# First self attention of a two-layer decoder: queries projected two units ahead, rotated sums rounded one unit later, written-out orders for VectorE and ScalarE

## The chip, the cores and the metric

One Trainium2 chip, one of its cores. The metric is device time in microseconds of one execution of the whole program. A core has a matmul engine (TensorE, in the profile PE, with its weight loads as PEld), VectorE (DVE), ScalarE (ACT), GpSimd (POOL) and SyncE (SP), each with a queue of its own that runs in order; they meet only by semaphores. DMA transfers are started from SyncE and GpSimd.

## What is computed

A decoder of two layers on x of 2 x 512 tokens of 512 features. Each sublayer is followed by adding its input and a layer norm. In order: causal self attention with rotary embedding (the subject here), cross attention to 1024 context rows with RMS norms, an expert MLP, causal self attention, grouped cross attention, and an MLP with weights and activations quantised to fp8 steps. All 16 heads have 128 features.

```python
q = split_heads(x @ Wq); k = split_heads(x @ Wk); v = split_heads(x @ Wv)
q = _apply_rope(q, cos, sin); k = _apply_rope(k, cos, sin)
scores = jnp.einsum('bhqd,bhkd->bhqk', q, k) * scale
scores = jnp.where(causal, NEG_INF, scores)
attn = jax.nn.softmax(scores, axis=-1)
ctx = jnp.einsum('bhqk,bhkd->bhqd', attn, v)
return ctx @ Wo
```

## The kernel before

Every product is made in float32 quality out of bfloat16 parts: an operand is kept as a high part and a low part (hi, lo), and `three()` issues three matmuls, hi by hi, hi by lo, lo by hi (lines 1272 to 1274). ScalarE writes a hi part as a rounded copy, VectorE the lo part as a difference.

**Units.** Attention goes by units: one head of one batch row, 32 in all, two batch rows of a head after each other. A unit has four quarters `qt` of 128 queries; since the mask is causal, quarter `qt` has 128 (qt + 1) keys. Its steps for a quarter: the score on TensorE into one of two score banks; VectorE adds mask and scale and takes the minimum (`scores`, L1187; it writes `p` and `nb`); ScalarE takes the exponential with its row sum (L892); VectorE the reciprocal (`inverse`, L1196); ScalarE the normalised hi part (`rounded`, L881, writes `phl`); VectorE its lo part (`remainder`, L1206); SyncE starts one DMA transpose of both (L463, it lands in `pT`, a part of `wo`), and TensorE multiplies them by v (`weigh`). `units()` (line 225) writes units 0 to 3 and 28 to 31 out and puts the 24 between in a loop of four.

**Jobs.** The projections of later units are jobs in slots between the quarters of a unit: `slots = [("Q",), ("K",), (), ("V",)]` (line 74). Their two banks in PSUM are taken in turn: a job waits for VectorE's part of the job two before it (`job_lo`). `lead(kind)` says how many units ahead a job works: before, 2 for K and 1 for Q and V. The rotation of a Q or K job passes through three engines: ScalarE copies the two halves of the bank crosswise to `swap` (L832, L833), VectorE multiplies the bank by the cosine into `rot` (L1143), GpSimd multiplies `swap` by the sine (L661) and adds it to `rot` (`rope`, L664, counted by `rope_sum`). Then `rotated` writes the hi part on ScalarE (L861, counted by `rope_hi`) and the lo part on VectorE (L1159, counted by `rope_lo`). Before, K's is done in the next unit, Q's at the end of quarter 1 of the same unit.

**Orders.** ScalarE and VectorE walk through the quarters with `unit()`, all by one pattern: VectorE does reciprocal of the last quarter, score, remainder of the last quarter, parts of the job; ScalarE does rounding of the last quarter, exponential, parts of the job. TensorE: score 0, Q, weighting of quarter 1 of the last unit, score 1, K, weighting of quarter 2, score 2, score 3, weighting of quarter 3, V, weighting of the unit's own quarter 0.

**Weights.** GpSimd splits raw weights into hi and lo: key and value weights of a head (`wkv`, L551 and L556) in quarter 0 of every odd unit, ahead of Q's rotation; the query weight (`wq`) in quarter 1, behind K's rotation (`split_plan`, line 91, and GpSimd's `unit`, line 671). The end of `wq_lo` counts `w_split`, for which the job of that head waits (`job`, line 1379: `pe.wait_ge(w_split, head(n + lead) + 1)`). SyncE loads the raw weights in even units, behind the transpose of quarter 0. From unit 29 on GpSimd splits the output weights `wo` instead.

## Time and profile before

| | before |
|---|---|
| median of 3 runs (lowest to highest) | 2615.45 us (2614.6 to 2620.56) |
| profiled execution, its own time | 2614.38 us |
| span of the profiled execution, first to last instruction | 2612.6 us |
| TensorE matmul busy | 2438.2 us (93%) |
| TensorE weight load busy | 1567.4 us (60%) |
| VectorE busy | 1848.3 us (71%) |
| ScalarE busy | 1588.8 us (61%) |
| GpSimd busy | 711.8 us (27%) |
| granted TensorE clock, mean | 0.976 |
| first score of unit 0 of the first self attention | 36.5 us |
| first score of its unit 31 | 435.0 us |

How to read the rows further down: times are microseconds from the first instruction; a timeline row has start, duration, engine, line, operation, output <- inputs with their shapes, and in brackets how long the engine had been idle before it and who ended that. A duration counts from when the engine began with the instruction, so a time in which it was held up inside is part of it. Names of tiles are those of the program without buffer numbers; `wo_hi<-phl` is a transposed softmax tile.

### The profile page before, as it was taken

The page shows a single profiled execution, that of the slowest core. Times are in us where ns is not written, and L with a number is a line of the kernel's source. Part 1 is how long each engine was busy: PE and PEld are TensorE (multiplying, and loading weights), DVE is VectorE, ACT ScalarE, POOL GpSimd, SP SyncE. Part 2 cuts the span into 40 slices and gives each one's busy share as a digit, 9 for nine tenths or more (in the row PEclk, how much of TensorE's full clock was granted, in tenths as well). Part 3 has the DMA queues.
Part 4 walks back from the last instruction along what each step waited for, and adds up shares of the span by engine and source line. Part 5 has one row for each costly group of instructions (what it writes and reads, how often), then busy time and mean ns, then how long its engine had stood idle before and what let it go on. Part 6 is the DMA issues. An engine that isn't in the chain of part 4 may idle for free. (4 is left out here: it accounts for less than half of the span.)

```text
span 2612.6 us, 57672 instructions
## 1 busy us (share of the span) xinstructions
PE 2438.2 (93%) x21584; PEld 1567.4 (60%) x21584; DVE 1848.3 (71%) x3371; ACT 1588.8 (61%) x2718; POOL 711.8 (27%) x671
## 2 busy tenths in 40 slices
PE   7999998989999999999988999999899999999864
PEld 4555555546666666666465666665566666665432
DVE  4777777657777777776665666667578888884597
ACT  5777675158887777886244566553277777773242
POOL 5666665601111111012332222226100000013111
PEclk9999999999999999999988999999999999999987
DMA  2433335325666666667341444445188777777200
GB/s 93 90 76 87 79 82 127 103 55 108 114 118 110 113 109 117 115 108 154 113 169 26 94 93 96 95 93 139 30 146 149 145 147 144 146 149 153 69 1 32
DMA packets 769429, 273.83 MB, mean 105 GB/s; under 512 B 737905, under 2 KB 740721, under 8 KB 767601
## 3 DMA queue, kind: packets, MB, share of 16 engines
q1 hardware_dynamic: 767504, 265.82, 49.0%
q0 software_dynamic: 1760, 5.77, 0.8%
q8 instruction: 110, 1.80, 0.3%
q14 instruction: 55, 0.44, 0.1%
HBM read 84.55 MB, written 6.44 MB: 35 GB/s over the span
## 5 line engine op out<-in xcount | busy, mean ns | idle before, releaser
L881 ACT ACTIVATE phl<-p,ri 128x1024 bf16<-128x1024 f32 (+4 forms) x512 | 437.4, 854 | 414.0 <-DVE ri L1196 386.1
L1206 DVE SCALAR_TENSOR_TENSOR phl<-p,ri,phl 128x1024 bf16<-128x1024 f32 (+4 forms) x512 | 514.1, 1004 | 103.3 <-issue 75.3
L892 ACT ACTIVATE p<-p,nb 128x1024 f32<-128x1024 f32 (+4 forms) x512 | 435.9, 851 | 53.9 <-DVE nb L1189 39.6
L1273 PE MATMUL ps<-wo_lo,v_hi 128*128 128x128 bf16 x2496 | 440.0, 220 | 0.0
L1272 PE MATMUL ps<-wo_hi,v_hi 128*128 128x128 bf16 x2240 | 396.5, 220 | 23.0 <-DMA wo_hi<-phl 15.7
L1274 PE MATMUL ps<-wo_hi,v_lo 128*128 128x128 bf16 x2240 | 396.2, 220 | 0.0
L1272 PE MATMUL ps<-k_hi,q_hi 128*128 128x512 bf16 (+3 forms) x768 | 272.5, 355 | 20.9 <-DVE nb L1187 18.7
L1273 PE MATMUL ps<-k_lo,q_hi 128*128 128x512 bf16 (+3 forms) x768 | 271.9, 354 | 0.0
L1274 PE MATMUL ps<-k_hi,q_lo 128*128 128x512 bf16 (+3 forms) x768 | 271.7, 354 | 0.0
L1273 PEld LDWEIGHTS ps<-wo_lo,v_hi 128*128 128x128 bf16 x2496 | 245.1, 98 | 33.4 <-issue 0.5
L1272 PEld LDWEIGHTS ps<-wo_hi,v_hi 128*128 128x128 bf16 x2240 | 219.5, 98 | 68.0 <-DMA wo_hi<-phl 27.9
L551 POOL TENSOR_SCALAR wkv_hi<-raw_kv 128x1024 bf16<-128x1024 f32 (+1 forms) x56 | 49.2, 878 | 658.9 <-PE ps L1274 509.5
L1274 PEld LDWEIGHTS ps<-wo_hi,v_lo 128*128 128x128 bf16 x2240 | 219.7, 98 | 0.0
L1272 PE MATMUL ps<-xT_hi,wq_hi 128*128 128x512 bf16 x512 | 195.1, 381 | 4.5 <-DVE xT_lo L958 3.5
L1191 DVE CUSTOM_DVE_ANT_0 p<-ps,rk,nq 128x1024 f32<-128x1024 f32 x128 | 163.1, 1274 | 51.3 <-PE ps L1274 51.0
L1273 PE MATMUL ps<-xT_lo,wq_hi 128*128 128x512 bf16 x512 | 195.1, 381 | 0.0
L1274 PE MATMUL ps<-xT_hi,wq_lo 128*128 128x512 bf16 x512 | 195.1, 381 | 0.0
L1272 PE MATMUL ps<-wo_hi,oT_hi 128*128 128x512 bf16 x512 | 194.4, 380 | 0.6 <-DVE nb L1187 0.6
L1273 PE MATMUL ps<-wo_lo,oT_hi 128*128 128x512 bf16 x512 | 194.2, 379 | 0.0
L1274 PE MATMUL ps<-wo_hi,oT_lo 128*128 128x512 bf16 x512 | 194.1, 379 | 0.0
L651 POOL TENSOR_TENSOR nq<-nq,half_neg 128x4 f32<-128x4 f32 x32 | 32.3, 1010 | 549.6 <-DVE nq L1140 549.6
L1189 DVE CUSTOM_DVE_ANT_0 p<-ps,mb 128x1024 f32<-128x1024 f32 x128 | 155.8, 1217 | 36.5 <-PE ps L1274 34.2
(200 smaller groups left out, 6126.5 us busy)
## 6 DMA issues: line engine op xcount, KB each, us to landing
raw_kv<-in_wkvself SPq DMA_DIRECT2D x32, 512.0 KB, 4.0
raw_q<-in_wqself SPq DMA_DIRECT2D x32, 256.0 KB, 2.6
raw_q<-in_woself SPq DMA_DIRECT2D x32, 256.0 KB, 2.8
raw_q<-in_wqcross SPq DMA_DIRECT2D x32, 256.0 KB, 3.0
raw_q<-in_wocross SPq DMA_DIRECT2D x32, 256.0 KB, 3.0
wo_hi<-phl SPq DMA_TRANSPOSE x384, 3.2
wo_lo<-phl SPq DMA_TRANSPOSE x384, 3.1
raw_kv<-in_wkvcross SPq DMA_DIRECT2D x24, 256.0 KB, 3.2
```

The costliest lines, as they stand in the source:

```text
L551: nc.gpsimd.tensor_scalar(hi, src, 1.0, 1.0, ALU.mult, ALU.mult).then_inc(w_hi, 1)
L651: nc.gpsimd.tensor_tensor(r, r, half_neg[:, 0:QT], ALU.pow).then_inc(q_norm, 1)
L881: nc.scalar.activation(m["ph"](qt, w), m["p"][:, qt % 2, 0:w], ACT.Copy, scale=ri[:, qt % 2:qt % 2 + 1]).then_inc(p_norm, 1)
L892: nc.scalar.activation(prob, prob, ACT.Exp, scale=1.0 if L.rms else -1.0, bias=nb[:, qt % 2:qt % 2 + 1], accum_out=rs[:, qt % 2:qt % 2 + 1 ...
L1189: ins = nc.vector.tensor_tensor_reduce(in1=m["mb"][:, L.batch(n), :], scale=-ISQ, op0=ALU.add, **kw)
L1191: ins = nc.vector.tensor_tensor_reduce(in1=m["rk"][:, n % 2, :], scale=m["nq"][:, n % 2, qt:qt + 1], op0=ALU.mult, **kw)
L1206: nc.vector.scalar_tensor_tensor(out=m["pl"](qt, w), in0=m["p"][:, qt % 2, 0:w], scalar=ri[:, qt % 2:qt % 2 + 1], in1=m["ph"](qt, w), op0= ...
L1272: nc.tensor.matmul(o, l(0), r(0), start=first, stop=False)
L1273: nc.tensor.matmul(o, l(0), r(1), start=False, stop=False)
L1274: return nc.tensor.matmul(o, l(1), r(0), start=False, stop=last)
```

## The change

In the first self attention alone (`L.rope`):

- `lead` is 2 for Q too: the job in unit n projects the queries of unit n + 2. The prologue (n = -2, -1) has one Q job more, unit 30 one less.
- `rotated` of both jobs is done in the next unit, on ScalarE and on VectorE. VectorE's cosine product waits first for the `rope_lo` of the unit before.
- ScalarE and VectorE get an order written out, `rotary_unit`, in place of the pattern.
- TensorE weighs quarter 1 of the last unit behind the unit's score 1 rather than ahead of it.
- GpSimd's and SyncE's programs stay as they are, apart from counts that follow from the lead.

```diff
--- before.py
+++ after.py
@@ -79,7 +79,7 @@
 
     def lead(self, kind):
 
-        return 2 if self.rope and kind in ("K",) else 1
+        return 2 if self.rope and kind in ("Q", "K") else 1
 
     def rope_count(self, n, qt):
 
@@ -880,23 +880,42 @@
                     act.wait_ge(r_inv, at(lambda n: c["s"] + QT * n + qt + 1, n, it))
                     nc.scalar.activation(m["ph"](qt, w), m["p"][:, qt % 2, 0:w], ACT.Copy, scale=ri[:, qt % 2:qt % 2 + 1]).then_inc(p_norm, 1)
 
+                def rotary_unit(n, it):
+
+                    if n:
+                        rounded(n - 1, it, 3)
+                    exponential(n, it, 0)
+                    rotated(n - 1, it, 0)
+                    job_parts(n, it, 0, L.jobs(n, 0))
+                    rounded(n, it, 0)
+                    exponential(n, it, 1)
+                    rotated(n - 1, it, 1)
+                    job_parts(n, it, 1, L.jobs(n, 1))
+                    exponential(n, it, 2)
+                    rounded(n, it, 1)
+                    exponential(n, it, 3)
+                    rounded(n, it, 2)
+                    job_parts(n, it, 3, L.jobs(n, 3))
+                    if n:
+                        heads_out(n - 1, it)
+
+                def exponential(n, it, qt):
+
+                    act.wait_ge(s_max, at(lambda n: CREDIT + c["s"] + QT * n + qt + 1, n, it))
+                    prob = m["p"][:, qt % 2, 0:L.width(qt)]
+                    if L.rms:
+                        nc.scalar.activation(nb[:, qt % 2:qt % 2 + 1], m["mx"][:, qt % 2:qt % 2 + 1], ACT.Copy, scale=-1.0).then_inc(max_neg, 1)
+                        act.wait_ge(max_neg, at(lambda n: QT * n + qt + 1, n, it))
+                    nc.scalar.activation(prob, prob, ACT.Exp, scale=1.0 if L.rms else -1.0, bias=nb[:, qt % 2:qt % 2 + 1], accum_out=rs[:, qt % 2:qt % 2 + 1]).then_inc(p_exp, 1)
+
                 def unit(n, it):
                     for qt in range(QT):
                         if n or qt:
                             rounded(*((n, it, qt - 1) if qt else (n - 1, it, QT - 1)))
-                        act.wait_ge(s_max, at(lambda n: CREDIT + c["s"] + QT * n + qt + 1, n, it))
-                        prob = m["p"][:, qt % 2, 0:L.width(qt)]
-                        if L.rms:
-                            nc.scalar.activation(nb[:, qt % 2:qt % 2 + 1], m["mx"][:, qt % 2:qt % 2 + 1], ACT.Copy, scale=-1.0).then_inc(max_neg, 1)
-                            act.wait_ge(max_neg, at(lambda n: QT * n + qt + 1, n, it))
-                        nc.scalar.activation(prob, prob, ACT.Exp, scale=1.0 if L.rms else -1.0, bias=nb[:, qt % 2:qt % 2 + 1], accum_out=rs[:, qt % 2:qt % 2 + 1]).then_inc(p_exp, 1)
-                        if L.rope and qt == 0:
-                            rotated(n - 1, it, 1)
+                        exponential(n, it, qt)
                         job_parts(n, it, qt, L.jobs(n, qt))
                         if qt == QT - 1 and n:
                             heads_out(n - 1, it)
-                        if L.rope and qt == 1:
-                            rotated(n, it, 0)
                         if L.rms:
                             key_norms(n, it, qt, L.jobs(n, qt))
 
@@ -907,11 +926,11 @@
                 for n in (-2, -1):
                     for qt in range(QT):
                         job_parts(n, None, qt, L.jobs(n, qt))
-                        if L.rope and (n == -2 or qt == 0):
+                        if L.rope and n == -2:
                             rotated(n, None, qt)
                         if L.rms:
                             key_norms(n, None, qt, L.jobs(n, qt))
-                units(act, unit, L)
+                units(act, rotary_unit if L.rope else unit, L)
                 rounded(UNITS - 1, None, QT - 1)
                 if L.name in EARLY:
                     act.wait_ge(p_lo, c["s"] + QT * UNITS)
@@ -1140,6 +1159,8 @@
                             nc.vector.tensor_scalar(m["nq"][:, u % 2, :], bank[:, 0:QT], 1.0, EPS * HD, ALU.mult, ALU.add).then_inc(job_lo, 1)
                         elif L.rope:
                             r = ("Q", "K").index(kind)
+                            if n > -2:
+                                dve.wait_ge(rope_lo, at(lambda n: c["rope"] + L.rope_count(n - 1, qt) + 1, n, it))
                             nc.vector.tensor_tensor(m["rot"][:, r, :], bank, m["cos"][:, :], ALU.mult).then_inc(job_lo, 1)
                         elif kind == "Q":
                             nc.vector.tensor_tensor(m["q"][1][:, u % 2, :], bank, m["q"][0][:, u % 2, :], ALU.subtract).then_inc(job_lo, 1)
@@ -1215,13 +1236,32 @@
                         job_parts(n, it, qt, L.jobs(n, qt), ("QN",))
                         if n or qt:
                             remainder(*prior)
-                        if L.rope and qt == 0:
-                            rotated(n - 1, it, 1)
                         job_parts(n, it, qt, L.jobs(n, qt), ("K", "KN", "Q", "V"))
                         if qt == QT - 1 and n:
                             heads_out(n - 1, it)
-                        if L.rope and qt == 1:
-                            rotated(n, it, 0)
+
+                def rotary_unit(n, it):
+
+                    scores(n, it, 0)
+                    if n:
+                        remainder(n - 1, it, 3)
+                    rotated(n - 1, it, 0)
+                    scores(n, it, 1)
+                    inverse(n, it, 0)
+                    job_parts(n, it, 0, L.jobs(n, 0))
+                    remainder(n, it, 0)
+                    scores(n, it, 2)
+                    rotated(n - 1, it, 1)
+                    job_parts(n, it, 1, L.jobs(n, 1))
+                    inverse(n, it, 1)
+                    remainder(n, it, 1)
+                    scores(n, it, 3)
+                    inverse(n, it, 2)
+                    remainder(n, it, 2)
+                    inverse(n, it, 3)
+                    job_parts(n, it, 3, L.jobs(n, 3))
+                    if n:
+                        heads_out(n - 1, it)
 
                 if L.rope:
                     dve.wait_ge(const_in, 32)
@@ -1235,10 +1275,11 @@
                 for n in (-2, -1):
                     for qt in range(QT):
                         job_parts(n, None, qt, L.jobs(n, qt))
-                        if L.rope and (n == -2 or qt == 0):
+                        if L.rope and n == -2:
                             rotated(n, None, qt)
-                units(dve, unit, L)
-                inverse(UNITS - 1, None, QT - 1)
+                units(dve, rotary_unit if L.rope else unit, L)
+                if not L.rope:
+                    inverse(UNITS - 1, None, QT - 1)
                 remainder(UNITS - 1, None, QT - 1)
                 quantise_run(EARLY.get(L.name, ()))
                 heads_out(UNITS - 1, None)
@@ -1434,12 +1475,12 @@
                             last = three(ps[:, S_BANK + 2 * (qt % 2) + half, 0:w], lambda k: m["q"][k][:, n % 2, qt * P:qt * P + P],
                                          lambda k: m["k"][k][:, L.kvslot(n), half * 512:half * 512 + w], True, True)
                         last.then_inc(s_mm, 1)
-                        if L.causal and qt == QT - 1 and n:
-                            weigh(n - 1, it, QT - 1)
+                        if L.causal and n and qt in (1, QT - 1):
+                            weigh(n - 1, it, qt)
                         for x, (kind, half) in enumerate(L.jobs(n, qt)):
                             job(n, it, qt, x, kind, half)
                         bn, bq = behind(n, qt, LAG)
-                        if bn >= 0 and not (L.causal and bq == QT - 1):
+                        if bn >= 0 and not (L.causal and bq in (1, QT - 1)):
                             weigh(bn, it, bq)
 
                 pe.wait_ge(x_lo, c["ln"] + NT)
```

## Rows read from the trace of the kernel before

**Rows 1.** Busy time by engine, the steady units of the stage.
```profile
core 0: us, PE busy (x) PEld busy (x) DVE busy (x) ACT busy (x) POOL busy (x), PEclk, DMA share, GB/s
60.00:407.00 347.00, 316.00 (x3086) 203.60 (x3084) 257.22 (x596) 246.25 (x544) 212.98 (x161) 1.00 0.36 81
```

**Rows 2.** Waits, 60 to 420 us: waiter, releaser, total, times, longest.
```profile
PEld ps L1272 <- DVE nb L1187: 27.7, 28, 1.2
ACT phl L881 <- DVE ri L1196: 98.7, 112, 1.4
```

**Rows 3.** Timeline of ScalarE in one unit.
```profile
203.93 0.39 ACT L892 ACTIVATE p<-p,nb 128x128 f32<-128x128 f32 x1
...
204.96 0.59 ACT L832 ACTIVATE swap<-ps 64x512 f32<-64x512 f32 x1
...
206.98 0.40 ACT L881 ACTIVATE phl<-p,ri 128x128 bf16<-128x128 f32 x1 [0.83 <-DVE ri L1196]
...
207.94 0.59 ACT L832 ACTIVATE swap<-ps 64x512 f32<-64x512 f32 x1
```

**Rows 4.** Timeline of VectorE in the same unit.
```profile
204.96 0.69 DVE L1159 TENSOR_TENSOR k_lo<-rot,k_hi 128x512 bf16<-128x512 f32 x1
...
209.82 1.21 DVE L1159 TENSOR_TENSOR q_lo<-rot,q_hi 128x512 bf16<-128x512 f32 x1
210.95 0.15 DVE L1196 RECIPROCAL ri<-rs 128x1 f32<-128x1 f32 x1
...
211.73 0.71 DVE L1206 SCALAR_TENSOR_TENSOR phl<-p,ri,phl 128x256 bf16<-128x256 f32 x1 [0.17 <-issue]
...
213.25 1.32 DVE L1206 SCALAR_TENSOR_TENSOR phl<-p,ri,phl 128x384 bf16<-128x384 f32 x1
...
215.94 0.27 DVE L1187 CUSTOM_DVE_ANT_0 p<-ps,causal_bias 128x128 f32<-128x128 f32 x1
```

**Rows 5.** Timeline of GpSimd, same unit, and the last query split of the loop.
```profile
209.21 1.27 POOL L661 TENSOR_TENSOR swap<-swap,sin 128x512 f32<-128x512 f32 x1 [0.27 <-ACT swap L833]
210.64 1.52 POOL L664 TENSOR_TENSOR rot<-rot,swap 128x512 f32<-128x512 f32 x1 [0.16 <-POOL swap L661]
212.13 0.79 POOL L551 TENSOR_SCALAR wq_hi<-raw_q 128x512 bf16<-128x512 f32 x1
213.00 1.16 POOL L556 TENSOR_TENSOR wq_lo<-raw_q,wq_hi 128x512 bf16<-128x512 f32 x1
...
392.15 1.16 POOL L556 TENSOR_TENSOR wq_lo<-raw_q,wq_hi 128x512 bf16<-128x512 f32 x1
```

**Rows 6.** Timeline of TensorE: first matmul of Q, of K, and the third score.
```profile
211.80 0.38 PE L1272 MATMUL ps<-xT_hi,wq_hi 128*128 128x512 bf16 x1
...
215.66 0.38 PE L1272 MATMUL ps<-xT_hi,wkv_hi 128*128 128x512 bf16 x1
...
218.75 0.33 PE L1272 MATMUL ps<-k_hi,q_hi 128*128 128x384 bf16 x1
```

**Rows 7.** Timeline, VectorE and GpSimd starting together in unit 29.
```profile
412.28 1.46 DVE L1206 SCALAR_TENSOR_TENSOR phl<-p,ri,phl 128x128 bf16<-128x128 f32 x1 [0.25 <-issue]
412.32 1.26 POOL L664 TENSOR_TENSOR rot<-rot,swap 128x512 f32<-128x512 f32 x1
```

**Rows 8.** Groups of VectorE by shape, 60 to 420 us: count, busy us, mean ns, idle before.
```profile
L1143 DVE TENSOR_TENSOR rot<-ps,cos 128x512 f32<-128x512 f32 x56 | 38.7, 691 | 45.7 <-ACT swap L833 45.5
L1187 DVE CUSTOM_DVE_ANT_0 p<-ps,causal_bias 128x384 f32<-128x384 f32 x28 | 14.9, 531 | 0.0
```

**Rows 9.** Timeline: remainder of quarter 0, then the key split of the next unit.
```profile
220.28 0.35 DVE L1206 SCALAR_TENSOR_TENSOR phl<-p,ri,phl 128x128 bf16<-128x128 f32 x1 [0.25 <-issue]
...
226.62 1.04 POOL L551 TENSOR_SCALAR wkv_hi<-raw_kv 128x1024 bf16<-128x1024 f32 x1 [1.69 <-DMA raw_kv<-in_wkvself]
227.75 2.13 POOL L556 TENSOR_TENSOR wkv_lo<-raw_kv,wkv_hi 128x1024 bf16<-128x1024 f32 x1
```

**Rows 10.** Timeline of VectorE: first score of unit 30 and of unit 31.
```profile
420.68 0.27 DVE L1187 CUSTOM_DVE_ANT_0 p<-ps,causal_bias 128x128 f32<-128x128 f32 x1
...
434.99 0.26 DVE L1187 CUSTOM_DVE_ANT_0 p<-ps,causal_bias 128x128 f32<-128x128 f32 x1
```

## The prediction

> **What bounds the kernel now.** I read the busy times first. In the steady part of the first self attention no engine is full: TensorE is busy 316 of 347 us, VectorE 257, ScalarE 246, GpSimd 213 [rows 1]. The waits then say who holds whom. Weight loads wait 27.7 us for a score's minimum on VectorE, and ScalarE waits 98.7 us, 112 times, for VectorE's reciprocal [rows 2]. So TensorE is fed late by two engines that wait for each other. The timeline shows how: in unit after unit VectorE stands behind a swap of ScalarE, then ScalarE behind the next reciprocal. Rows of ScalarE [rows 3] and VectorE [rows 4] give the steps. The split of a query weight recurs from 213.00 to 392.15 in seven pairs of units [rows 5], 25.59 us a pair, 12.80 a unit.
>
> TensorE alone could do a unit in about 11.1: three projections of 12 x 512 columns and 7680 columns of scores and weighting. A projection is 12 matmuls in 2.6 us: key projection to the third score is 215.66 to 218.75, 3.09 with 0.5 of weighting in it [rows 6]. So 1.7 a unit is the most that can be won, about 50 us over the loop.
>
> **A second limit that the order must meet.** GpSimd and VectorE shut each other out where VectorE reads two tensors of SBUF. k_lo takes 0.69 with GpSimd idle; q_lo, of the same form, takes 1.21 at 209.82, of which 0.66 pass until GpSimd's product is over (209.21 + 1.27) [rows 4, 5]. The remainder of 384 columns started at 213.25 beside the split of 213.00 and took 1.32, ending 0.41 after it. GpSimd pays too: its sum took 1.52 at 210.64, its twin elsewhere 1.26 [rows 5, 7]. Who asks first wins, and at a near tie GpSimd does: at 412.28 a remainder of 128 columns asked 0.04 ahead of GpSimd's sum and took 1.46, to 0.16 past the sum's end [rows 7]. Rotations and splits keep GpSimd busy 213 of 347 us [rows 1], so this matters most when the loop gets tighter.
>
> The Trainium skill says the same (SBUF — State Buffer, section Who interferes with whom): a VectorE instruction with two SBUF inputs contends with a GpSimd instruction that reads SBUF, and the pair is an exclusive lock held for the whole instruction. It speaks against this change, which tightens two engines' orders and leaves GpSimd's alone; by port sharing at half speed instead, each collision would cost a part of what I charge below.
>
> **Part 1: the ping-pong.** The new orders put the swap of one projection, the rounding and the next exponential side by side. No instruction is added or removed in a steady unit, only its turn. Laid out from a unit's first score at 0, all inputs ready (a score takes 0.3 to 0.7, the one of 384 columns 0.53, a cosine 0.69 [rows 8]): exponential at 0.3, swap of Q at 1.3 (203.93 to 204.96 is 1.03 [rows 3]), swap over at 2.6, rounding and exponential 0.9 (206.98 to 207.94), k_hi 0.64, swap of K at 4.1 to 5.3, cosine and reciprocal at 5.9, remainder of 256 at 6.7 (210.95 to 211.73 is 0.78 [rows 4]), score 512 at 7.1, its exponential at 7.9, remainder 384 at 9.3, next unit at 11.1. Without collisions this would meet TensorE's 11.1: the change would win everything.
>
> **Part 2: collisions in a unit with splits (odd n).** GpSimd multiplies Q's swap 1.27 after the swap's start (207.94 to 209.21), at 2.6 to 3.9, adds at 4.0 to 5.3. The remainder of 128 asks at 3.2 and ends at 4.0; score 384 to 4.55; k_lo asks at 4.55 behind the sum and runs 5.1 to 5.8; reciprocal 6.3, remainder 256 asks at 7.10. K's product, held by k_lo, runs 5.65 to 6.9 and its sum asks at 7.08. It wins, by the near tie above; remainder 8.1 to 8.6, score 512, exponential 9.3, rounding 10.0, remainder 384 10.7 to 11.35, next unit's first score at 12.6. So 1.5 of the 1.7 goes back.
>
> **Part 3: the weight split.** With a lead of two, Q of an even unit needs the query weight that GpSimd splits in the odd unit before it, behind K's rotation. GpSimd's order is unchanged. Before, Q began at 211.80 while that split ended at 213.00 + 1.16 = 214.16 [rows 5, 6]: K waited for it then, at 215.66 or later, and had 1.5 to spare; Q would have been late by 2.4. In the new order the sum of K ends at 8.35 and the split (212.13 to 214.16, 2.03 [rows 5]) at 10.35; TensorE would have been there at about 8.2. Q, score, weighting, K, weighting, score 384 are 7.0 from there, so score 384 is ready at 17.35 and VectorE takes it at 17.5 (it would have wanted it at 16.6).
>
> **Part 4: the even unit.** Its K swap starts at 12.6 + 4.1 = 16.7, its product asks at 17.98; k_lo, behind the late score, asks at 18.05 and loses: 19.05 to 19.75, cosine to 20.35, sum 20.4 to 21.65, remainder 256 to 21.95, remainder 384 asks at 24.05. The raw weights land 5.99 after the end of the remainder of 128 (220.28 + 0.35 to 226.62 [rows 9]); that end is now 16.65, so the key weight's split runs 22.65 to 23.7 and its second half (2.13) asks at 23.8, ahead of the remainder by 0.25. Remainder to 26.3, next pair at 27.6 (1.37 later, as 213.25 + 1.32 to 215.94). Where weights land 0.3 later the remainder wins and the pair takes 26.1. I take 26.9, nearer the first, since its order follows from the rows as they stand: 1.3 more than 25.6.
>
> **Edges.** The prologue rotates one projection more before the first score: between nothing, if it is hidden, and a whole rotation (swap 1.2, product 1.27, sum 1.26, rounding 0.6, in all 4.3); I take 3.6, since a wait of TensorE overlaps it. Unit 30 has no Q job any more; it took 434.99 - 420.68 = 14.3 [rows 10] and goes to about 11.5. Units 28 and 29 have no splits: 12.1 each with the collisions of part 2 in one of two, for 12.8. In all 4.2 less; with a shorter last unit 6. I take 6, between 2 and 8. W of quarter 1 moves behind the second score: its input lands before, so nothing; if its cover is gone at most the 0.4 of one weighting a unit. The wait added on VectorE (rope_lo) stands behind rotated() on the same engine and is met: nothing. Transposes keep their queue order on SyncE. After the loop TensorE works through, so what is lost there reaches the end.
>
> **Sum.** 14 pairs x 1.3 = 18.2, + 3.6, - 6 = 15.8. The profiled execution took 2614.4, its span 2612.6 (the table above); the median of the runs is 1.05 above it. 2615.45 + 15.8 = 2631.
>
> **Rivals.**
> Near ties go to VectorE (faster). Each of three decisions above is by 0.02 to 0.25 us. If k_lo gets ahead of the product at 18.0, the even unit saves 1.1; if remainder 384 is ahead of the key weight's second half, 1.6 more; if remainder 256 is ahead of the sum, 1.0. With all of them the pair is about 24.4: 14 x -1.2 - 2.4 = -19, 2596. It decides at 0.1 us earlier for k_lo. For it: the remainder of 220.28 ran unhindered in 0.35, between GpSimd's product and its sum [rows 9]. Against: GpSimd is busy 61% of the time.
> They split (no change): some ties go one way and some the other, the pair takes 25.3 to 25.9, 2609 to 2617.
> TensorE bound: collisions hide behind ScalarE and the split comes in time: 14 x (22.4 - 25.6) = -45, 2570. Against it: the 2.4 of part 3 and q_lo's 0.52 in every unit of before.
> The change leaves the ping-pong as it is, waits of ScalarE for reciprocals near 98.7 us again: then only edges and splits remain, 2613 to 2620; it has its chance within that of no change.
>
> By the Trainium skill's word that issue order and not an operation's shape decides who blocks (same page and section), the rival of the near ties is real: the order of requests alone separates 2596 from 2640.
>
> **How the numbers follow.** Forecast (slower) 0.50; ties to VectorE 0.27; no change 0.18; TensorE bound 0.05. Its own range is 2620 (pair 26.1) to 2641 (pair 27.6), both with edges of -2.4, and 2646 with 0.4 more for the weighting of quarter 1 in some twelve units. To leave out no more than 2 in 10 I go down to the ties' rival: 2594 to 2646. Measurement can tell about 0.3%, 7.8 us, from no change: faster 0.32, same 0.18, slower 0.50.
>
> **What would show it.** In the changed profile: (1) weight loads waiting for GpSimd's wq_lo ahead of the Q projection, about 2 us each second unit; (2) the wait of ScalarE for reciprocals far below 98.7; (3) remainders of 256 and k_lo of 1.2 us and more, as durations, not as idle; (4) wq_lo starts 26.9 apart; (5) TensorE busy about the same in microseconds, less as a share. I am wrong if remainders and k_lo stay near their free times (0.35 for 128 columns [rows 9], 0.69 for k_lo), or if wq_lo starts come 25 or less apart.

## The result, and the profile after

The changed kernel takes 2651.84 us (median; 2647.52 to 2658.31) against 2615.18 of the kernel before: a ratio of 1.0131, 95% interval 1.0116 to 1.0146. It is slower by 36.7 us, where 15.8 were forecast: the sign was right, the size lies outside the range. The profiled execution took 2652.94 with a span of 2650.8, 38.2 more than before. In all that follows one execution ran at a lower granted clock (0.836 on the mean; 2915.99 us, the kernel of experiment 11) and is left out.

The page of after, first lines (span; busy time, share and instructions of TensorE, weight loads, VectorE, ScalarE, GpSimd):

```profile
span 2650.8 us, 57734 instructions
PE 2443.8 (92%) x21584; PEld 1575.5 (59%) x21584; DVE 1868.3 (70%) x3371; ACT 1586.0 (60%) x2718; POOL 709.2 (27%) x671
```

Where it went, by first scores of units 0, 28 and 31 (VectorE's timeline; start, duration):

```profile
40.72 0.28 DVE L1208 CUSTOM_DVE_ANT_0 p<-ps,causal_bias 128x128 f32<-128x128 f32 x1
...
431.28 0.28 DVE L1208 CUSTOM_DVE_ANT_0 p<-ps,causal_bias 128x128 f32<-128x128 f32 x1
...
469.17 0.28 DVE L1208 CUSTOM_DVE_ANT_0 p<-ps,causal_bias 128x128 f32<-128x128 f32 x1
```

Before, these stood at 36.54, 395.08 and 434.99. So the prologue costs 4.2, the 28 units 390.56 - 358.54 = 32.0, which is 2.29 a pair, and the last units give back 39.91 - 37.89 = 2.0: 34.2 in all. The first normalisation behind the layer is 34.7 late (first mean at 500.14 before, 534.80 after). The other 3.5 of the span arise in later layers, whose instructions didn't change: from that normalisation to the end it is 2112.5 before and 2116.0 after. The same stretch, with the same instructions, took 2111.3 to 2119.0 in the profiled executions of all kernels of this document, so 3.5 lies within what it varies by.

The starts of the query weight's second half, GpSimd's timeline, which in [rows 5] were 25.59 apart:

```profile
65.88 1.16 POOL L556 TENSOR_TENSOR wq_lo<-raw_q,wq_hi 128x512 bf16<-128x512 f32 x1
93.09 1.16 POOL L556 TENSOR_TENSOR wq_lo<-raw_q,wq_hi 128x512 bf16<-128x512 f32 x1
...
427.77 1.16 POOL L556 TENSOR_TENSOR wq_lo<-raw_q,wq_hi 128x512 bf16<-128x512 f32 x1
```

13 pairs in 361.89 are 27.84 a pair, between 27.2 and 28.5. The waits of the loop (window 60 to 440; engine, line, releaser: us, times, longest), against [rows 2]:

```profile
ACT p L909 <- DVE nb L1208: 77.4, 68, 2.4
DVE phl L1227 <- issue: 55.6, 55, 1.4
ACT phl L881 <- DVE ri L1217: 47.5, 42, 1.9
PE ps L1313 <- POOL wq_lo L556: 32.3, 14, 2.6
PEld ps L1313 <- DVE v_lo L1154: 22.9, 13, 2.5
POOL rot L664 <- DVE rot L1164: 20.1, 14, 1.5
```

The ping-pong in its old form is gone: ScalarE's wait for reciprocals fell from 98.7 to 47.5, the weight loads' wait for the minima nb is out of the list. But ScalarE doesn't wait less for VectorE: its exponentials now wait 77.4 for the minima, so the two together are 124.9. And TensorE has two new waits: 2.3 us a pair for the weight split, and one that the prediction hadn't named: K of the odd units waits for v_lo, the end of a VectorE queue that is late. The groups of VectorE in the same window (busy us, mean ns | idle before) show why it is late:

```profile
L1180 DVE TENSOR_TENSOR k_lo<-rot,k_hi 128x512 bf16<-128x512 f32 x28 | 38.7, 1381 | 0.0
L1227 DVE SCALAR_TENSOR_TENSOR phl<-p,ri,phl 128x384 bf16<-128x384 f32 x27 | 30.7, 1139 | 36.9 <-issue 36.9
L1227 DVE SCALAR_TENSOR_TENSOR phl<-p,ri,phl 128x256 bf16<-128x256 f32 x28 | 30.1, 1077 | 18.6 <-issue 18.6
L1227 DVE SCALAR_TENSOR_TENSOR phl<-p,ri,phl 128x128 bf16<-128x128 f32 x27 | 22.2, 821 | 1.2 <-ACT phl L881 1.2
L1180 DVE TENSOR_TENSOR q_lo<-rot,q_hi 128x512 bf16<-128x512 f32 x27 | 18.7, 693 | 10.8 <-ACT q_hi L861 10.8
```

Same instructions, same sizes, longer: k_lo 1.38 where it was 0.69 [rows 4]. q_lo is free now; k_lo and the remainders of 128, 256 and 384 columns behind it pay (0.34, 0.49 and 0.63 in experiment 3, where GpSimd is out of the way).

One pair in full, VectorE's rows and then GpSimd's. Odd unit from 251.14, even from 263.92, the next from 278.62:

```profile
251.14 0.28 DVE L1208 CUSTOM_DVE_ANT_0 p<-ps,causal_bias 128x128 f32<-128x128 f32 x1
...
263.92 0.28 DVE L1208 CUSTOM_DVE_ANT_0 p<-ps,causal_bias 128x128 f32<-128x128 f32 x1
...
269.29 1.74 DVE L1180 TENSOR_TENSOR k_lo<-rot,k_hi 128x512 bf16<-128x512 f32 x1
...
275.73 1.71 DVE L1227 SCALAR_TENSOR_TENSOR phl<-p,ri,phl 128x384 bf16<-128x384 f32 x1 [1.37 <-issue]
278.62 0.28 DVE L1208 CUSTOM_DVE_ANT_0 p<-ps,causal_bias 128x128 f32<-128x128 f32 x1
```

```profile
260.42 1.16 POOL L556 TENSOR_TENSOR wq_lo<-raw_q,wq_hi 128x512 bf16<-128x512 f32 x1
...
269.22 1.27 POOL L661 TENSOR_TENSOR swap<-swap,sin 128x512 f32<-128x512 f32 x1
...
274.90 2.13 POOL L556 TENSOR_TENSOR wkv_lo<-raw_kv,wkv_hi 128x1024 bf16<-128x1024 f32 x1
```

In the frame of the prediction (0 at 251.14): wq_lo ends at 10.44 (forecast 10.35), K's product asks at 18.08 (17.98), k_lo at 18.15 (18.05) and loses, the key weight's second half asks at 23.76 (23.8), remainder 384 behind it at 24.59 (24.05), next pair at 27.48 (27.6). These are the steps of the upper of the two branches of part 4.

Some pairs are a microsecond longer. Two pairs before, TensorE stood still until wq_lo ended, and then its clock fell. TensorE's row, then windows (columns: length, busy us and instructions by engine, granted clock, DMA share, GB/s):

```profile
205.69 0.55 PE L1313 MATMUL ps<-xT_hi,wq_hi 128*128 128x512 bf16 x1 [2.49 <-POOL wq_lo L556]
```

```profile
203.00:205.60 2.60, 0.21 (x4) 0.03 (x1) 1.70 (x4) 0.81 (x3) 2.52 (x3) 1.00 0.15 31
205.70:209.30 3.60, 3.60 (x9) 1.28 (x10) 2.83 (x7) 2.97 (x7) 0.00 (x0) 0.53 0.32 62
209.40:213.00 3.60, 3.60 (x24) 1.94 (x23) 2.63 (x6) 2.60 (x6) 1.39 (x2) 1.00 0.38 73
```

For 3.6 us the clock was at its 1.2 GHz level; 9 matmuls are recorded there, 24 in the same length behind it. Q took 4.3 instead of 2.6. This happened behind 4 of the 14 waits for wq_lo (in front of Q of units 10, 12, 24 and 26); from first score to first score those pairs are 28.3 to 28.5 long, against 27.4 to 27.6 for most others. One more pair took 28.2 at a granted clock of 1.00: there the raw key weights landed 0.7 later, and remainder 384 took 2.42.

### The profile page after: what moved, and what is told of

It reads as the page before. It is cut to its first block and busy times, and to the rows that moved or that the text cites. A ratio compares the mean times of both kernels' runs of the same rounds, so it can differ in the third digit from the quotient of the medians.

```text
span 2650.8 us, 57734 instructions
## 1 busy us (share of the span) xinstructions
PE 2443.8 (92%) x21584; PEld 1575.5 (59%) x21584; DVE 1868.3 (70%) x3371; ACT 1586.0 (60%) x2718; POOL 709.2 (27%) x671
## 5 line engine op out<-in xcount | busy, mean ns | idle before, releaser
L1227 DVE SCALAR_TENSOR_TENSOR phl<-p,ri,phl 128x1024 bf16<-128x1024 f32 (+4 forms) x512 | 535.1, 1045 | 136.8 <-issue 109.5
L1313 PE MATMUL ps<-xT_hi,wq_hi 128*128 128x512 bf16 x512 | 198.7, 388 | 42.8 <-POOL wq_lo L556 32.3
```

Of the source, the lines that this page charges most:

```text
L1227: nc.vector.scalar_tensor_tensor(out=m["pl"](qt, w), in0=m["p"][:, qt % 2, 0:w], scalar=ri[:, qt % 2:qt % 2 + 1], in1=m["ph"](qt, w), op0= ...
L1313: nc.tensor.matmul(o, l(0), r(0), start=first, stop=False)
```

## The experiments

Shares of the loss are told per pair of units, by the starts of wq_lo: 25.59 before, 27.84 after, 14 pairs. Each group of experiments was compared with executions of the kernel before that ran with it (medians 2614.85 for 1 to 4, 2618.18 for 5 to 8, 2617.33 for 9 to 11, 2619.36 for 12). The times of 2, 3, 4, 7, 8 and 11 are of one execution each; the changed kernel's own four lie between 2647.52 and 2658.31. The diffs are cut to the lines that matter.

**1. The query split ahead of K's rotation** (on the changed kernel):

```diff
 # GpSimd's unit
-                        if L.rope and qt:
+                        if L.rope and qt > 1:
                             rope(n, it, qt, L.jobs(n, qt))
...
-                        if L.rope and qt == 0:
+                        if L.rope and qt < 2:
                             rope(n, it, qt, L.jobs(n, qt))
```

> The changed kernel, with GpSimd's split of the query weight moved ahead of K's rotation (quarter 1 of odd units). Weight-split theory: the wait of TensorE for wq_lo (2.3 us, 14 times) goes, and with it the stretch at half clock behind it (granted clock 0.53 for 3.6 us, some 1.7 us lost each time); wq_lo starts 25.5 to 26.3 apart in place of 27.8, the whole 2610 to 2630. Collision theory (VectorE and GpSimd shutting each other out is what costs, the late query is incidental): collisions stay, starts stay above 27, the whole above 2640.

2622.64, ratio 1.0032 (1.0015 to 1.0048): the time as forecast. TensorE no longer waits for wq_lo, and 29 of the 36.7 us come back. What is left is VectorE's lateness; weight loads, same window:

```profile
PEld ps L1313 <- DVE v_lo L1154: 27.5, 22, 2.7
```

Its executions spread from 2616.4 to 2638.2, and the profiled one is the slowest, with 26.6 a pair. The rows show what can spread them: in the even units remainder 384 and the key weight's second half are now mostly asked for within 0.15 us of each other, and the unit takes 12.6 to 13.0 or 14.6 to 14.7. Two such meetings:

```profile
264.21 0.62 DVE L1227 SCALAR_TENSOR_TENSOR phl<-p,ri,phl 128x384 bf16<-128x384 f32 x1 [1.37 <-issue]
...
369.55 2.54 DVE L1227 SCALAR_TENSOR_TENSOR phl<-p,ri,phl 128x384 bf16<-128x384 f32 x1 [1.37 <-issue]
```

```profile
264.27 2.54 POOL L556 TENSOR_TENSOR wkv_lo<-raw_kv,wkv_hi 128x1024 bf16<-128x1024 f32 x1
...
369.56 2.12 POOL L556 TENSOR_TENSOR wkv_lo<-raw_kv,wkv_hi 128x1024 bf16<-128x1024 f32 x1
```

VectorE won where it was 0.06 ahead and lost where it was 0.01 ahead. It lost in 8 of 13 even units; behind 7 of these TensorE stood still for v_lo for 2.3 to 2.5 us, the granted clock fell, and the odd unit took 13.0 instead of 12.0. So a loss costs up to 2.9 us a pair (27.7 against 24.8). That more meetings were won in the other executions would explain their times, but only one has a trace.

**2. TensorE kept busy while it waits** (on the changed kernel), 11 matmuls into an unused bank:

```diff
+                    if kind == "Q" and L.rope and n >= 2 and n % 2 == 0:
+                        for f in range(FILL):
+                            nc.tensor.matmul(ps[:, 1, :], xT[0][:, f % XC, 0:P], xT[0][:, f % XC, 0:512], start=True, stop=True)
                     if kind in ("Q", "K", "V"):
```

> The changed kernel, with 11 matmuls of 512 columns into an unused bank of PSUM in front of TensorE's wait for the query weight in even units (2.4 us of work inside a wait of 2.6). Clock theory: the granted clock stays at 1.0 behind the wait, the Q projection takes 2.6 us in place of 4.3, and a pair of units falls by about 1.6 us to 26.2, the whole to about 2628. Rival, the late start of Q alone counts and the clock is hidden behind ScalarE and VectorE: the pair stays at 27.8 within 0.3, the whole at 2648 to 2655.

2647.14, which is 4.7 below the changed kernel's median and within 0.4 of its fastest execution: the rival held. Q's window behind the wait:

```profile
285.40:288.10 2.70, 2.67 (x13) 1.25 (x14) 2.18 (x7) 2.07 (x5) 0.00 (x0) 1.00 0.17 36
```

The clock stays at 1.00 behind all 14 of these waits and Q takes 2.6, yet a pair takes 27.68. The 28 units take 386.79, 3.8 less than without the filler, although the clock now fell at three other places, in front of K of an odd unit (waits for v_lo of 1.66 to 2.48). The four longer pairs of the changed kernel's profile say the same, about 1 us each. So the fallen clock behind this wait is some 4 us of 36.7; the late start costs more.

**3 and 4. GpSimd out of the way**, in the changed kernel (3) and in the kernel before (4): its rotation and loop splits cut to one column each.

```diff
-                        nc.gpsimd.tensor_tensor(m["swap"][:, r, :], m["swap"][:, r, :], m["sin"][:, :], ALU.mult).then_inc(rope_mul, 1)
+                        nc.gpsimd.tensor_tensor(m["swap"][:, r, 0:1], m["swap"][:, r, 0:1], m["sin"][:, 0:1], ALU.mult).then_inc(rope_mul, 1)
...
+                if tiny:
+                    hi, lo, src = hi[:, 0:1], lo[:, 0:1], src[:, 0:1]
```

> The changed kernel with GpSimd's rotation products and sums and its weight splits in the loop cut to one column each; left out are the sine part of the rotation and the split of all but the first two heads' weights, every wait stays. Collision and split theories together: nothing shuts VectorE out and no weight is late, so the loop goes down to TensorE's own work, 22.3 to 23 us a pair, the whole 2560 to 2580. Rival, the new orders of ScalarE and VectorE hold each other up by themselves: 25 or more a pair, above 2605.

> The kernel before with the same cut of GpSimd's work (same parts left out). If the ping-pong of ScalarE and VectorE is what bounds it, as I read it, only the collisions' share of about 1 us a unit goes: 23 to 24.4 a pair, the whole 2580 to 2600, and the written-out order is then worth 0.5 to 1.5 us a pair over it. Rival, collisions bound it as well: 22.4 a pair, level with the changed kernel.

2573.51 for the changed kernel, 2595.56 for the one before, pairs of 22.45 and 24.55. The changed kernel's groups:

```profile
L1229 DVE SCALAR_TENSOR_TENSOR phl<-p,ri,phl 128x384 bf16<-128x384 f32 x28 | 17.7, 632 | 38.3 <-issue 38.3
L1182 DVE TENSOR_TENSOR k_lo<-rot,k_hi 128x512 bf16<-128x512 f32 x28 | 19.2, 687 | 0.0
```

So the new order is worth 22 us where GpSimd does next to nothing: a unit of 11.2, the 11.1 of part 1. (The cut takes away three things at once: the collisions, the late weight, and the time that GpSimd's own work takes. Experiments 1, 7 and 10 help to part them.) Both times are as forecast; a pair of the old order, 24.55, is just above its 24.4. GpSimd's work then costs the old order 2615.2 - 2595.6 = 19.6 and the new one 2651.8 - 2573.5 = 78.3. By the group means, GpSimd lengthened VectorE's instructions by 2 x (0.52 + 0.33 + 0.19 + 0.17 + 0.09) = 2.6 us a pair before (q_lo, then the remainders of 384, 256, 128 and 512 columns) and by 2 x (0.69 + 0.51 + 0.59 + 0.48) = 4.5 after (k_lo, then 384, 256 and 128). The old order hid more than half of it, 25.59 against 24.55 a pair; the new one costs 5.4 a pair.

**5. The lead alone**, without the written-out orders (on the kernel before): Q is projected two units ahead in the old pattern, both halves are taken in the next unit.

```diff
-        return 2 if self.rope and kind in ("K",) else 1
+        return 2 if self.rope and kind in ("Q", "K") else 1
 # ScalarE and VectorE
-                        if L.rope and qt == 0:
-                            rotated(n - 1, it, 1)
+                        if L.rope and qt < 2:
+                            rotated(n - 1, it, qt)
...
-                        if L.rope and qt == 1:
-                            rotated(n, it, 0)
```

> The kernel before with the lead of two for Q and both roundings of rotated sums in the next unit, but in the old pattern of ScalarE and VectorE, and TensorE's order as before. Split theory: Q of even units waits 2 to 2.5 us for wq_lo, which the ping-pong hides in part: pairs of 25.6 to 26.7, the whole 2615 to 2632. Rival, the written-out orders bring nothing good or bad and the lead alone makes the loss: pairs of 27.5 or more, 2645 or above. Rival, the lead alone helps since q_lo leaves its collision with GpSimd: pairs under 25.3, below 2611.

2629.08, ratio 1.0038 (1.0027 to 1.005), pairs of 26.4, as forecast. Both troubles are there, the reciprocals' ping-pong and the weight split:

```profile
ACT phl L881 <- DVE ri L1196: 103.0, 116, 1.3
PE ps L1270 <- POOL wq_lo L556: 33.2, 14, 2.7
```

The wait for the split comes from the lead and not from the written-out orders. The same wait costs less here, 0.8 a pair. Why was not taken apart: q_lo is out of its collision (0.69), but k_lo takes 1.02 and remainder 256 takes 1.04 on the mean.

**6. K rotated directly behind Q** (on 1), so k_lo runs ahead of GpSimd's product:

```diff
 # VectorE; ScalarE likewise
                     rotated(n - 1, it, 0)
+                    rotated(n - 1, it, 1)
                     scores(n, it, 1)
...
                     scores(n, it, 2)
-                    rotated(n - 1, it, 1)
```

> The changed kernel with the query split moved ahead as in e1_early_split, and K's rotated sum rounded directly behind Q's on ScalarE and VectorE, at the start of the unit, where GpSimd rotates nothing. Collision theory: k_lo runs in 0.69 in place of 1.38 and the near tie of k_lo with K's product is gone; pairs of 23.5 to 25.2 for 26.7 in e1, the whole 2580 to 2605, faster than both kernels. Rival, other collisions (remainders of 256 and 384 columns) fill the room: pairs stay at 26 or more, 2612 or above.

2614.3, ratio 0.9982 (0.9972 to 0.9991): the forecast 2580 to 2605 was missed, but this is the first order that isn't slower than before. A pair takes 25.4, between forecast and rival: even units 11.4, odd ones 13.8 to 14.7. What an odd unit loses (VectorE, then GpSimd):

```profile
281.55 2.56 DVE L1227 SCALAR_TENSOR_TENSOR phl<-p,ri,phl 128x512 bf16<-128x512 f32 x1
...
284.63 1.75 DVE L1180 TENSOR_TENSOR k_lo<-rot,k_hi 128x512 bf16<-128x512 f32 x1
```

```profile
281.43 2.13 POOL L556 TENSOR_TENSOR wkv_lo<-raw_kv,wkv_hi 128x1024 bf16<-128x1024 f32 x1
...
284.48 1.35 POOL L661 TENSOR_TENSOR swap<-swap,sin 128x512 f32<-128x512 f32 x1 [0.92 <-ACT swap L833]
```

The remainder came 0.12 behind the key weight's second half and lost 1.8, which made k_lo come 0.15 behind the product. One lost tie makes the next.

**7. Only the splits cut to one column** (on the changed kernel, the last two lines of the diff of 3).

> The changed kernel with only the weight splits of the loop cut to one column (left out: the split of all but the first two heads' weights), the rotation on GpSimd whole. If the splits are the larger part of what GpSimd costs here (late query weight, clock, and the hold of the 384 remainder): 24.5 to 25.5 a pair, that is two thirds of the way from 27.8 to the 22.45 of e3_after_free; 2600 to 2618. Rival, the rotation's collisions are the larger part: 26 or more.

2618.19, pairs of 25.57, every unit 12.8: just outside the forecast. So of the 5.4 a pair that GpSimd costs the new order, the splits cost 2.3 (27.84 to 25.57) and the rotation 3.1 (25.57 to 22.45). The 2.3 still leaves out some of the wait for the query weight: its split stands behind K's rotation here too, and Q of the even units still waits 1.1 for it.

**8. The weighting of quarter 1 ahead of score 1 again** (on the changed kernel).

```diff
-                        if L.causal and n and qt in (1, QT - 1):
+                        if L.causal and n and qt == QT - 1:
...
-                        if bn >= 0 and not (L.causal and bq in (1, QT - 1)):
+                        if bn >= 0 and not (L.causal and bq == QT - 1):
```

> The changed kernel with TensorE's weighting of quarter 1 back ahead of score 1 in place of behind it. Taken as costing nothing in the prediction: pairs of 27.8 within 0.4, 2645 to 2658. Rival, it matters, since TensorE waits for the transpose and score 1 comes late to VectorE: 28.3 or more a pair, above 2660.

2647.55, pairs of 27.7: this part costs nothing, as predicted.

**9. The key weight's second half last** (on 6), behind K's sum; its rounding stays first, and TensorE's count of split weights moves to it. (Here and in 10 and 12 the diff is shortened to GpSimd's list.)

```diff
 # pieces of quarter 0 and 1 in odd units: (ahead of the rotation, behind it)
-{0: [("kv", 0), ("kv", 1)], 1: [("q", 0), ("q", 1)]}
+[([("kv", 0)], []), ([("q", 0), ("q", 1)], [("kv", 1)]), ([], []), ([], [])]
...
-                    split_lo(lo, src, hi, item, kind == "q")
+                    split_lo(lo, src, hi, item, kind == closing)   # closing: "kv" in this loop
```

> The kernel with K's halves directly behind Q's, and GpSimd's order in odd units changed further: the rounding of the key weights stays first, then Q's product and sum, the query split, K's product and sum, and the low half of the key weights (2.13 us) last instead of first. Theory (collisions with GpSimd's two-input instructions are the price, and what counts is which VectorE instruction meets them): the remainder 512, which took 2.56 us behind that low half, and k_lo, which took 1.75, are freed; the low half ends about 12.3 us into the unit, and the next unit's remainder 512 loses at most 0.7 us to it, so a pair falls from 25.4 us to 24 to 24.8 and the time to 2590 to 2606. Rival (VectorE's total time lost is the same wherever GpSimd's instructions stand, since both are nearly full in a unit): pairs stay at 25.2 to 25.8 and the time at 2609 to 2620.

2672.73, ratio 1.021 (1.0193 to 1.0227), pairs of 29.5. Both theories missed. VectorE was freed as hoped (remainder 512 0.94, k_lo 0.68 on the mean), but since the count moved, Q of the even unit waited for the key weight:

```profile
271.99 0.61 PE L1321 MATMUL ps<-xT_hi,wq_hi 128*128 128x512 bf16 x1 [4.86 <-POOL wkv_lo L558]
```

TensorE wanted Q at 267.1, 8.1 after the odd unit's first score at 259.01, which part 3 had said (8.2) and this expectation forgot. It waits 59.4 us, 13 times, and the granted clock is 0.50 behind the wait shown (272.00 to 276.00). A pair is 4.1 longer than in 6: nearly all of the 4.6 that TensorE waits.

**10. The key weight's second half in the middle** (on 6): behind Q's sum, ahead of the query split; the count stays with the query.

```diff
-{0: [("kv", 0), ("kv", 1)], 1: [("q", 0), ("q", 1)]}
+[([("kv", 0)], [("kv", 1)]), ([("q", 0), ("q", 1)], []), ([], []), ([], [])]
```

> The same, but the low half of the key weights stands directly behind Q's sum, ahead of the query split, so K's product and sum come last. Theory: it runs from about 5.8 to 7.9 us of the unit, where remainder 256 meets it (blocked by about 1.1 us, in a stretch with some 1.4 us of idle VectorE behind it); the query split ends at 9.7, and K's sum at 12.3 against the next unit's remainder 512 (0.7 lost). Pair 24 to 24.8, time 2590 to 2606. Rival as for the kernel with the low half last: 25.2 to 25.8, 2609 to 2620.

2598.9, ratio 0.9931 (0.9912 to 0.995), as forecast: faster than both kernels, with a pair of 24.2 (even units 11.4, odd 12.8). It computes all that the reference does. Its group of k_lo, and the wait it still has:

```profile
L1188 DVE TENSOR_TENSOR k_lo<-rot,k_hi 128x512 bf16<-128x512 f32 x29 | 20.8, 717 | 0.0
```

```profile
PE ps L1321 <- POOL wq_lo L558: 21.1, 14, 1.8
```

**11. Shorter instructions** (on the changed kernel): each product and sum of the rotation in two halves of 256 columns.

```diff
-                        nc.gpsimd.tensor_tensor(m["swap"][:, r, :], m["swap"][:, r, :], m["sin"][:, :], ALU.mult).then_inc(rope_mul, 1)
+                        nc.gpsimd.tensor_tensor(m["swap"][:, r, 0:256], m["swap"][:, r, 0:256], m["sin"][:, 0:256], ALU.mult)
+                        nc.gpsimd.tensor_tensor(m["swap"][:, r, 256:512], m["swap"][:, r, 256:512], m["sin"][:, 256:512], ALU.mult).then_inc(rope_mul, 1)
```

> The changed kernel with each of GpSimd's products and sums of the rotation cut into two instructions of 256 columns; nothing else. Theory (a VectorE instruction is held until the end of the one GpSimd instruction that is under way, so the length of a single instruction sets each loss): k_lo falls from 1.38 us to about 1.0 on the mean and the remainders by 0.2 to 0.3, a pair of units from 27.84 to 26.2 to 27.2, the time to 2625 to 2645. Rival (the two engines share a rate, or a held VectorE instruction is beaten again by the second half): k_lo stays at 1.3 us or more and the time at 2648 to 2660, the second instructions' own start-up included.

2651.69, pairs of 27.9: the rival's time, but by the theory's mechanism. VectorE lost less:

```profile
L1182 DVE TENSOR_TENSOR k_lo<-rot,k_hi 128x512 bf16<-128x512 f32 x27 | 22.4, 828 | 0.0
L1229 DVE SCALAR_TENSOR_TENSOR phl<-p,ri,phl 128x256 bf16<-128x256 f32 x27 | 21.1, 780 | 18.0 <-issue 18.0
L1229 DVE SCALAR_TENSOR_TENSOR phl<-p,ri,phl 128x384 bf16<-128x384 f32 x27 | 37.4, 1385 | 36.9 <-issue 36.9
```

k_lo 0.83 against 1.38 (0.69 in the odd units from 7 on, 0.93 to 0.94 in the even ones, where it ends 0.55 behind the product's first half as it ended 0.54 behind the whole product), the remainder of 128 columns 0.34 against 0.82. But a rotation now takes GpSimd 0.73 + 0.89 + 0.82 + 0.77 = 3.2 instead of 1.37 + 1.28 = 2.65, so wq_lo ends later; TensorE waits for it 40.3 us (14 times, longest 3.3) instead of 32.3, and remainder 384 is worse off (1.39). Gain and loss cancel.

**12. The query split ahead of the key weight's second half, with counts of their own** (on 10): Q waits for the query's count, K and V for the key's.

```diff
-[([("kv", 0)], [("kv", 1)]), ([("q", 0), ("q", 1)], []), ([], []), ([], [])]
+[([("kv", 0)], []), ([("q", 0), ("q", 1), ("kv", 1)], []), ([], []), ([], [])]
...
+                        if L.rope and kind != "Q":
+                            pe.wait_ge(kv_split, at(lambda n: L.head(n + lead) + 1, n, it))
+                        else:
                             pe.wait_ge(w_split, at(lambda n: c["split"] + L.head(n + lead) + 1, n, it))
```

> The kernel with the key weights' low half behind Q's sum, with one more move: the query split stands ahead of that low half, and K's and V's products wait for a count of their own, so Q's product waits for the query split alone. In the last kernel TensorE waited 1.8 us a pair for wq_lo, whose end was at 280.65 where Q was wanted at 278.9. Theory (the time follows the place of the weight split and of the collisions): the query split ends at about 278.3 and costs TensorE nothing; the key weights end at about 280.4, ahead of K's product; K's sum ends 1.3 us earlier in the pattern, but still meets the next remainder 512, which loses up to 0.9. Pair of units 24.2 us before, now 23.0 to 23.7; 14 pairs give 2582 to 2592. Rival (TensorE's wait only moves to K's product or to the values nb, since GpSimd and VectorE are both full in odd units): pairs at 24.0 to 24.4, time 2595 to 2603.

2600.35, ratio 0.9932 (0.9916 to 0.9949), pairs of 24.4: the rival held. The wait for wq_lo is gone, and others took its place (weight loads, window 60 to 407):

```profile
PEld ps L1323 <- DMA wo_lo<-phl: 20.3, 28, 2.4
PEld ps L1323 <- DVE v_lo L1164: 11.0, 12, 1.2
```

The first is the transfer that turns the remainders phl, and v_lo stands behind remainder 384 in VectorE's order; that remainder now meets the key weight's second half (1.00 on the mean, 0.84 in 10). What bounds an odd unit now is not shown. Neither GpSimd nor VectorE is full, as the expectation had it: of the 13.0 us of the odd unit from 248.75 to 261.75, GpSimd is busy 9.7, VectorE 10.2 and TensorE 12.2.

## Why the prediction was right, and where it was wrong

**Part 1, the ping-pong: right.** With GpSimd out of the way the unit takes 11.2 for 11.1 forecast (3), and the new order alone is worth 22 us. The wait for reciprocals halved. Not foreseen: ScalarE's exponentials wait for the minima instead (77.4), even in 3 (57.1 in the window 60 to 380), where the unit took no longer for it.

**Part 2, collisions in an odd unit: right.** Forecast 12.6 from first score to first score, measured 12.8 in the steady units. k_lo asks at 4.66 of the unit (forecast 4.55) and remainder 256 at 7.43 (7.10), each behind an instruction of GpSimd; with GpSimd's work cut away (3) the 1.5 a unit comes back. The Trainium skill's rule (SBUF — State Buffer, section Who interferes with whom: an exclusive lock for the whole instruction, issue order decides) agrees, but for near ties of up to 0.04 us (last section): a held instruction ends 0.4 to 0.55 us after GpSimd's end (k_lo at 271.03, the product at 270.49; remainder 384 at 277.44, the key weight at 277.03), and with GpSimd's instructions halved k_lo ended the same 0.55 behind a half (11). Sharing at half speed would give neither a fixed distance from GpSimd's end nor a gain from a cut.

**Part 3, the weight split: right in place, short in price.** It forecast TensorE at 8.2 and the split at 10.35; the rows have 8.1 and 10.4 to 10.5, and the waits 32.3 us in 14 pairs. It wasn't in the forecast that TensorE's clock could fall behind such a wait: some 4 us by the rows and by experiment 2. The lead causes this wait by itself (5), moving the split removes it (1).

**Part 4, the even unit: the step that failed.** The sum has 14 x 1.3 for it, a pair of 26.9; measured are 27.84 and 32.0 us for the 28 units. Both branches were worked out from rows, 27.6 and 26.1, and the text said that the order of the first "follows from the rows as they stand"; then it took 26.9, for weights that land 0.3 later. The pair shown above ran through the first branch to within 0.1 us at the requests listed with it but remainder 384, which asked 0.5 later (24.59 for 24.05) and still ended where forecast, at 26.3. So its distance to the key weight's second half was 0.83 and not 0.25, and weights 0.3 later could not turn it: they came 0.7 later once, and it lost. In none of the 13 even units with a key split did the other branch occur. It did once in experiment 2, in unit 14, where the weights landed 1.1 later, the second half stood at 12.02 of the unit and the remainder at 11.81: that pair took 26.4, for 26.1 forecast. With 27.5 the loop costs 14 x 1.9 = 27, with the clock 31, against 18.2 in the sum and 32.0 measured.

**Edges: half wrong.** The prologue cost 4.2 for 3.6. The last units gave 2.0 instead of 6, the other term that was mis-sized: unit 28 took 13.7 instead of 12.1, because its query weight is still split in unit 27 and TensorE waits for it there too; unit 29 took 12.6, unit 30 11.6 (11.5 forecast). The "shorter last unit" (1.8) doesn't exist: from the first score of unit 31 to the first normalisation it is 65.63 for 65.15 before. The weighting of quarter 1 cost nothing, as said (8).

**Sum.** Forecast 18.2 + 3.6 - 6 = 15.8; measured 32.0 + 4.2 - 2.0 = 34.2, and 38.2 in the span with what came later. Of the 18.4 between the first two 13.8 are the pair, 4.6 the edges. The mechanisms and the sign were right, and not by luck: their steps stand in the rows. The size was not.

**Rivals.** Near ties to VectorE: no; in the changed kernel GpSimd won at remainder 384 in each of the 13 even units with a key split, and at k_lo in 12 of them; but in 1 the meeting with the key split was not lost in 5 of 13. (This rival's own sum is off: 27.6 less its savings of 1.1, 1.6 and 1.0 is 23.9 and not 24.4.) TensorE bound: the pair of 22.4 came only without GpSimd's work (3, 22.45). No change and an unchanged ping-pong: no. **What would show it:** the signs came, with 27.84 for 26.9 in the fourth, and the third only in part: k_lo took 1.38 on the mean, but remainder 256 took 1.2 and more in the odd units only (1.28 to 1.34) and 0.86 to 0.93 in most even ones.

What stays open: with the splits cut (7) every unit runs through the rows of the changed kernel's odd unit (k_lo 1.22 at 4.7, remainder 256 at 7.4 taking 1.3, 12.8 in all), which is what part 2 had worked out for the rotation's collisions alone; that the old order also took 12.8 a unit looks like chance, and no run shows more.

## What to carry to other kernels

When a stage is freed of one chain of waits, ask which engine's instructions will then meet at the same memory, and which preparation now has an earlier deadline, and lay both out in order of requests: here a new order worth 22 us lost 59 more to GpSimd's work than the old one did, in collisions and in a weight that came late. A written-out order should cover all engines that take part: orders on VectorE and ScalarE were changed and GpSimd's left alone, and the version that moves GpSimd's steps with them (10) is 0.7% faster than before. When two branches of a forecast hang on one meeting and the rows as they stand give one, take that one rather than a value between, and ask whether the errors of the steps before it (here 0.5 us) are smaller than the distance that decides (0.25).

## What the runs showed of the hardware

- The loss of one collision is set by who asks first, down to 0.07 us: k_lo at 269.29 behind the product at 269.22 took 1.74, and remainder 512 at 281.55, behind a split at 281.43, took 2.56 for 0.75. VectorE won a meeting that it had asked for 0.06 earlier (264.21 and 264.27 in experiment 1) and lost two in which it was recorded 0.01 and 0.04 earlier (369.55 and 369.56 there; [rows 7]). No such lengthening shows in VectorE instructions that read one operand from PSUM: the score of 384 columns took 0.56 and the cosine 0.69 with GpSimd busy or idle.
- A held VectorE instruction ends a fixed time behind GpSimd's: k_lo 0.54 to 0.55 (0.69 when free), whether GpSimd's instruction takes 1.27 or 0.73, and remainder 384 0.41 (0.63 when free).
- After TensorE had stood still for about 2.5 us the granted clock fell (0.53 over the next 3.6 us in the case shown) behind 4 waits and stayed at 1.00 behind 6 others of 2.46 to 2.56 us; 11 matmuls in the gap kept it at 1.00 behind all 14 waits.
- Cutting an instruction of GpSimd of 512 columns (1.27 us free) into two of 256 (0.73 each) costs about 0.2 us (2 x 0.73 - 1.27).
